# A selective-scan kernel: softplus operations moved by a step, one product with B moved from GpSimd to VectorE, and D times u written by ScalarE instead of TensorE

## The chip, the cores and the metric

The kernel runs on one core of one Trainium2 chip. The metric is the time of one execution on the device in microseconds (us); a kernel's time is the median of its runs. TensorE is the matmul engine, VectorE, ScalarE and GpSimd are the elementwise engines, and SyncE (SP) issues the DMAs. In rows of the profile they are PE (PEld for weight loads), DVE, ACT, POOL and SP.

## The reference, cut to what matters

The input is 4 images of 512 channels of 24 x 24. After a norm over the channels each image becomes a sequence of 2304 steps with 128 channels, one learned token ahead of it, and goes through a Mamba block: 256 inner channels, 16 states each. The second part normalizes again, mixes 8 routed memory blocks into the first 128 tokens and adds.

```python
xz = jnp.einsum('bld,ed->ble', seq, in_proj_w)
u, z = jnp.split(xz, 2, axis=-1)
u = sum((up[:, k:k + L, :] * conv_w[:, k] for k in range(D_CONV))) + conv_b
u = jax.nn.silu(u)
x_dbl = jnp.einsum('bld,ed->ble', u, x_proj_w)
dt, Bm, Cm = jnp.split(x_dbl, [DT_RANK, DT_RANK + D_STATE], axis=-1)
dt = jax.nn.softplus(jnp.einsum('blr,dr->bld', dt, dt_proj_w) + dt_proj_b)
A = -jnp.exp(A_log)

def step(h, inputs):
    dt_t, B_t, C_t, u_t = inputs
    dA = jnp.exp(dt_t[:, :, None] * A)
    h = dA * h + (dt_t * u_t)[:, :, None] * B_t[:, None, :]
    y = jnp.einsum('bdn,bn->bd', h, C_t)
    return (h, y)
...
y = ys.transpose(1, 0, 2) + u * D
y = y * jax.nn.silu(z)
return jnp.einsum('bld,ed->ble', y, out_proj_w)
...
x = x + _L0_conv_ref(_ln_c(x), ...)
t = _to_tokens(x)
t = t + _L0_ffn_ref(_ln_t(t), ...)
```

## The kernel before

**Units and steps.** The work is cut into 24 units: 6 chunks of 4 image rows (384 sequence steps, `T`) times 4 images. The partitions hold 128 channels, and the 256 inner channels lie in two halves, so a tile is 128 x 384 or, for both halves, 128 x 768. Every engine has its own program, written out by hand as 16 steps `s` for each unit `J`, one for each state `n`. In the steps of unit `J` the state work of that unit runs, and beside it the preparation of unit `J + 1` ("front": projections, softplus), the end of unit `J - 1` ("back": output projection, second norm, store) and the first norm of unit `J + 3` ("norm"). Each engine works through its own list in order, and semaphores tie them.

**A state's way through the engines.** ScalarE writes the decay exp(dt A) of each half to `DA` in PSUM (L510) after the scan of that half of the state before it is done, since there is one buffer; states 1 and 2 have theirs written ahead, to `DAS1` and `DAS2` (L518). The drive, dt u times B, is made in one of two ways. For most states TensorE spreads B's row over the partitions into one of two `BB` buffers (L748), one or two steps ahead, and VectorE multiplies (L1057). For `POOL_STATES` = 3, 5, 7, 9 GpSimd does it (L450, in step `n - 2`), from `BS`, which a DMA fills once a unit (`load_b`). VectorE runs the scan of both halves (L1092) in step `n`. In step `n + 1` GpSimd multiplies the states by C (L442), which DMAs bring in groups of four states (`load_c`). In step `n + 3` (`LAG`) TensorE adds the product into `Yp` (L766).

**The turn of the unit.** State 15's product is GpSimd's in step 0 of the next unit and TensorE's in step 2. In step 2 VectorE forms `VV`, `Yp` times silu(z) (L1068), which empties `Yp`; only then may TensorE start the next unit's sum, in step 3. D times u is added to `Yp` by TensorE in step 10, with a diagonal matrix `DD` (L772).

**Softplus.** ScalarE does it in steps 6 to 10 (L589 to L606, absolute value, exp, ln, square, ln) and raises `log_ready`. GpSimd waits for that in step 10 and multiplies `SE` by `SR` (L455); in step 11, after C's product of state 10, it makes dt (L463) and dt times u (L465), and before them XC2 times `RSTD2` (L458), the last product of the second norm. In step 12 it adds the residual (L468), in step 15 it runs the first norm of a later unit (L425).

**The other work of TensorE in the last steps.** In step 12 it projects z (L889), which ScalarE copies from `PP` to `ZB` (L618); the convolution of unit `J + 2` (L907) in steps 13 to 15 uses the same banks and waits for that copy. For the unit before, the output projection (L791, L794) runs in step 3, ScalarE copies it (L546), a mean follows in step 5 (L799), VectorE subtracts it into `XC2` (L1132), ScalarE squares that in step 7 (L621), and TensorE takes the variance in step 8 (L809).

**The last units.** In unit 21 the router's scores are computed (L814, L825, L1102 and others); in units 22 and 23 the routed blocks are mixed by TensorE (L847).

SP issues in every unit: `load_c` for states 4 to 7, the write of the next unit's B and C rows to DRAM, `load_c` for 8 to 11 and 12 to 15, `load_b` and the first `load_c` of the next unit, and the store of the unit before. Each `load_c` waits for the products that free its half of the ring (the one for states 12 to 15 for that of state 7).

Of the kernel before, what the change touches and what calls it, by code (L numbers as in the profile page):

```python
# [11 lines left out]
ACT = mybir.ActivationFunctionType  # L12
ALU = mybir.AluOpType
# [27 lines left out]

FIT_X, FIT_V, FIT_S, FIT_A, FIT_K = 0.50996051, -3.6873482, -0.046276752, 0.88316448, 0.72962086
FIT_BIAS = (1.0, FIT_V, FIT_A, math.log(FIT_K))
POOL_STATES = (3, 5, 7, 9)
NPOOL = len(POOL_STATES)
NDVE = NS - NPOOL
HRING, MRING, CRING = 8, 4, 8
# [20 lines left out]
def build(nc, x, tok, w_in, conv_w, conv_b, xp_w, dt_w, dt_b, a_log, dvec, op_w, mem, router, out):  # L68
    ctx = ExitStack()
    with ctx:  # L70
# [118 lines left out]
        da_ready = sem("da_ready"); das_ready = sem("das_ready"); scan_done = sem("scan_done"); car_saved = sem("car_saved")  # L189
        m_ready = sem("m_ready"); ysum_done = sem("ysum_done")  # L190
        z_ready = sem("z_ready"); z_copied = sem("z_copied")
        gz_ready = sem("gz_ready"); v_ready = sem("v_ready")
        op_ready = sem("op_ready"); x2_ready = sem("x2_ready")
        mean2_ready = sem("mean2_ready"); xc2_ready = sem("xc2_ready"); sq2_ready = sem("sq2_ready")
        var2_ready = sem("var2_ready"); ln2_done = sem("ln2_done"); rstd2_ready = sem("rstd2_ready")
# [82 lines left out]
        def _(sp):  # L278
# [36 lines left out]
            def load_b(unit, p):  # L315

                sp.wait_ge(rows_written, 16 * (unit + 1))
                rows = ROWS_D[p, POOL_STATES[0]:POOL_STATES[-1] + 1:2]
                sp.dma_start(BS[:, :, :], rows.unsqueeze(0).broadcast_to([P, NPOOL, T])).then_inc(bs_loaded, 16)

            def store(c, b, k):
# [68 lines left out]
        @block.gpsimd  # L390
        def _(pool):
            pool.memset(DTNAT, 0.0).then_inc(zeroed, 1)
            pool.memset(MEANW[:, :], 1.0 / DIM).then_inc(const_ready, 1)
            pool.memset(IDENT[:, :], 0.0).then_inc(zeroed, 1)
            pool.memset(EPSC[:, :], EPS_C).then_inc(const_ready, 1)
            pool.memset(EPST[:, :], EPS_T).then_inc(const_ready, 1)
            pool.memset(LOGB[:, 0:1], 2.0 / LOG_C).then_inc(const_ready, 1)
            pool.memset(LOGB[:, 1:2], -LOG_G).then_inc(const_ready, 1)
            for i, v in enumerate(FIT_BIAS):
                pool.memset(FITB[:, i:i + 1], v).then_inc(const_ready, 1)  # L400
            pool.wait_ge(zeroed, 2)
            pool.affine_select(out=IDENT[:, :], in_=IDENT[:, :], compare_op=ALU.not_equal, fill=1.0,
                               base=0, pattern=[[-1, P]], channel_multiplier=1).then_inc(ident_ready, 1)
            pool.memset(XDT0[:, :], 1.0).then_inc(const_ready, 1)
            pool.memset(XDT[:, :], 1.0).then_inc(const_ready, 1)
            pool.memset(ONE4[:, :], 1.0).then_inc(const_ready, 1)
            for b in range(BATCH):
                pool.memset(XN[:, b * SLOT:b * SLOT + HIST - 1], 0.0).then_inc(const_ready, 1)

            pool.memset(SEL[:, :, :], 0.0).then_inc(zeroed, 1)  # L410
            for part in range(PARTS):
                pool.wait_ge(zeroed, 3 + part)
                pool.affine_select(out=SEL[:, :, :], in_=SEL[:, :, :], compare_op=ALU.not_equal, fill=1.0,
                                   base=-part * BC, pattern=[[-1, NS], [0, P]], channel_multiplier=1)\
                    .then_inc(zeroed if part < PARTS - 1 else sel_ready, 1)

            pool.wait_ge(w_loaded, 16 * N_WLOADS)
            for b in range(BATCH):
                pool.tensor_copy(XN[:, b * SLOT + HIST - 1:b * SLOT + HIST], TKC).then_inc(const_ready, 1)

            def normalize(g):

                pool.wait_ge(rstd_ready, g + 1)
                for r1 in range(2):
                    pool.tensor_tensor(seq_rows(unit_seq(g), r1), by_row_parity(XC[:, :, :], r1),  # L425
                                       by_row_parity(over_q(RSTD[:, :]), r1), ALU.mult).then_inc(xn_part, 1)
                pool.wait_ge(xn_part, 2 * (g + 1))
                pool.tensor_copy(XN[:, ds((g + BATCH) * SLOT, HIST)],
                                 XN[:, ds(g * SLOT + T, HIST)]).then_inc(xn_ready, 1)

            def step(J, par, s, main, front, back, prev, conv, norm):
                f, k, g, N = J + 1, J - 1, J + 3, NS * J + s
                fp = kp = 1 - par
                if main and (s > 0 or prev) or (s == 0 and prev):

                    n1 = (s - 1) % NS
                    unit1 = J if s else J - 1
                    g1 = n1 // GRP
                    pool.wait_ge(scan_done, 2 * N)
                    pool.wait_ge(c_loaded[g1 % 2], 16 * (GROUPS // 2 * unit1 + g1 // 2 + 1))  # L440
                    positive(pool, ysum_done, N - MRING)
                    pool.tensor_tensor(M[:, n1 % MRING], HB[:, n1 % HRING],  # L442
                                       over_halves(CS[:, n1 % CRING]), ALU.mult).then_inc(m_ready, 1)
                if main and s + 2 in POOL_STATES:

                    n2 = s + 2
                    pool.wait_ge(bs_loaded, 16 * (J + 1))
                    pool.wait_ge(dtu_ready, J + 1)
                    pool.wait_ge(car_saved, 4 * BATCH + 4 * J + (n2 - HRING) // GRP + 1)
                    pool.tensor_tensor(HB[:, n2 % HRING], DTU[:, par], over_halves(BS[:, pool_index(n2)]),  # L450
                                       ALU.mult).then_inc(dbu_pool, 1)
                if front and s == 10:

                    pool.wait_ge(log_ready, f + 1)
                    pool.tensor_tensor(SE[:, :, :], SE[:, :, :], SR[:, :, :], ALU.mult).then_inc(tail_done, 1)  # L455
                if back and s == 11:
                    pool.wait_ge(rstd2_ready, k + 1)
                    pool.tensor_tensor(XC2[:, :, :], XC2[:, :, :], over_q(RSTD2[:, :]), ALU.mult)\  # L458
                        .then_inc(xh2_done, 1)
                if front and s == 11:  # L460
                    pool.wait_ge(tail_done, f + 1)
                    pool.wait_ge(relu_done, f)
                    pool.tensor_tensor(DT[:, fp], DT[:, fp], SE[:, :, :], ALU.subtract).then_inc(dt_ready, 1)  # L463
                    pool.wait_ge(dt_ready, f + 1)
                    pool.tensor_tensor(DTU[:, fp], DT[:, fp], U[:, fp], ALU.mult).then_inc(dtu_ready, 1)  # L465
                if back and s == 12:
                    pool.wait_ge(xh2_done, k + 1)
                    pool.tensor_tensor(unit_seq(k).rearrange("p (q t) -> p q t", q=Q), XC2[:, :, :], unit_x(k),  # L468
                                       ALU.add).then_inc(out_ready, 1)
                if norm and s == 15:  # L470

                    normalize(g)

            normalize(0)
            normalize(1)
            normalize(2)
            run_units(pool, step)


        @block.scalar  # L480
        def _(act):
# [39 lines left out]
            def step(J, par, s, main, front, back, prev, conv, norm):  # L521
# [17 lines left out]
                if norm and s == 10:  # L539
                    act.wait_ge(xc_ready, g + 1)  # L540
                    positive(act, var_ready, g)
                    act.activation(SQ[:, :, :], XC[:, :, :], ACT.Square).then_inc(sq_ready, 1)
                if back and s == 4:

                    act.wait_ge(op_ready, k + 1)
# [69 lines left out]
                if main and s == z_step(J, norm) + (0 if norm or at(J, ROUTE) else 1):  # L615

                    act.wait_ge(z_ready, J + 1)
                    act.activation(ZB[:, :, :], PPT, ACT.Copy).then_inc(z_copied, 1)  # L618
                if back and s == 7:
                    act.wait_ge(xc2_ready, k + 1)  # L620
                    act.activation(SQ2[:, :, :], XC2[:, :, :], ACT.Square).then_inc(sq2_ready, 1)  # L621
                if back and s == (11 if main and not norm and not front or at(J, COMB - 1) else 9):
                    act.wait_ge(var2_ready, k + 1)
                    act.activation(LNV2[:, :], STAT2, ACT.Ln, bias=EPST[:, 0:1]).then_inc(ln2_done, 1)
# [114 lines left out]
        def _(pe):  # L739
# [4 lines left out]
            def spread_b(unit, par, n):  # L744

                before = NDVE * unit + dve_index(n)
                positive(pe, dbu_dve, before - 1)
                pe.matmul(BB[:, dve_index(n) % 2, 0:T], SEL[:, n], PT[:, par], start=True, stop=True)\  # L748
                    .then_inc(b_ready, 1)

            def step(J, par, s, main, front, back, prev, conv, norm):
# [7 lines left out]
                if main and s >= LAG or prev and s < LAG:  # L759

                    n3 = (s - LAG) % NS
                    pe.wait_ge(m_ready, N - LAG + 1)
                    if s == LAG:
                        positive(pe, v_ready, J)
                    for h in range(HALVES):
                        last = pe.matmul(Yp[:, h, 0:T], IDENT[:, :], M[:, n3 % MRING, h],  # L766
                                         start=n3 == 0, stop=n3 == NS - 1)
                    last.then_inc(ysum_done, 1)
                if main and s == 10:

                    for h in range(HALVES):
                        pe.matmul(Yp[:, h, 0:T], DD[:, h], U[:, par, h], start=False, stop=False)  # L772

                if front and s == 2:

# [255 lines left out]
        def _(dve):  # L1031
# [19 lines left out]
            def drive(unit, par, n, N):  # L1051
# [2 lines left out]
                product = DA[:, :, 0:T] if n in AHEAD else HB[:, n % HRING]  # L1054
                dve.wait_ge(car_saved, 4 * BATCH + 4 * unit + (n - HRING) // GRP + 1)
                dve.wait_ge(b_ready, NDVE * unit + dve_index(n) + 1)
                dve.tensor_tensor(product, DTU[:, par], over_halves(BB[:, dve_index(n) % 2, 0:T]), ALU.mult)\  # L1057
                    .then_inc(dbu_dve, 1)

            def step(J, par, s, main, front, back, prev, conv, norm):  # L1060
# [160 lines left out]
```

## Time and profile before

| | before |
|---|---|
| median of 3 runs | 1181.12 us (1179.61 to 1181.26) |
| the profiled execution's own time | 1184.08 us |
| its span, first to last instruction | 1181.9 us |
| busy: POOL, PE, DVE, ACT | 1062.0, 1043.8, 1024.6, 806.7 us |
| mean granted TensorE clock | 0.971 of full |

Times in rows are us from the span's start unless marked ns. A timeline row gives the start, the duration, the engine, the line, the operation, output and inputs, the count of instructions merged into the row, and in brackets how long the engine was idle before it and what ended that. Elementwise instructions of one engine overlap a little, so that the step from start to start is shorter than a duration.

### The profile page before, as it was taken

How to read it: one execution, taken by the hardware profiler on the slowest of the kernel's cores; microseconds unless marked ns; L12 is line 12 of the kernel's file. 1: busy time of each engine (PE TensorE's matmuls, PEld its weight loads, DVE VectorE, ACT ScalarE, POOL GpSimd, SP SyncE). 2: the span in 40 equal slices, each digit the busy share in tenths (PEclk: the TensorE clock that was granted, in tenths of full speed). 3: DMA queues.
4: the chain of work that ended last, by engine and by line, in shares of the span. 5: the costliest groups of instructions: out<-in, count | busy, mean ns of one | idle time of the engine just before them, and what ended most of it. 6: DMA issues, size and time to landing. Idle time of an engine off the chain costs nothing.

```text
span 1181.9 us, 13090 instructions
## 1 busy us (share of the span) xinstructions
PE 1043.8 (88%) x3786; PEld 616.3 (52%) x3786; DVE 1024.6 (87%) x1173; ACT 806.7 (68%) x1486; POOL 1062.0 (90%) x700
## 2 busy tenths in 40 slices
PE   6889889989998898898899899988988988987987
PEld 4545555555554555555555555555555555544554
DVE  3799898898898898998988988989989889888784
ACT  4677677677676776776766766767767767657653
POOL 3599999999999999999999999999999999978774
PEclk9799999999999999999999999999999999989999
DMA  6223132222322222221322223222322223245441
GB/s 177 93 97 108 63 114 82 89 80 89 115 82 88 95 102 89 88 108 63 114 76 96 82 87 114 82 89 87 109 89 88 105 66 123 87 142 175 154 141 28
DMA packets 64537, 116.78 MB, mean 99 GB/s; under 512 B 34218, under 2 KB 47954, under 8 KB 64466
## 3 DMA queue, kind: packets, MB, share of 16 engines
q1 hardware_dynamic: 64466, 115.96, 29.6%
q8 instruction: 30, 0.49, 0.2%
q14 instruction: 41, 0.34, 0.1%
HBM read 108.47 MB, written 7.47 MB: 98 GB/s over the span
## 4 chain that ended last, share of the span: by engine, by line
POOL 39%; PE 28%; issue 21%; DVE 10%; ACT 1%; POOLq 1%; DMA 0%; DVEq 0%; SPq 0%; ACTq 0%
POOL SCAN L442 28%; PE Yp L766 14%; DVE SCAN L1092 7%; PE PP L907 7%; POOL SCAN L450 6%; POOL UDT L463 3%; PE PP L847 2%; POOL XC L458 2%; DVE SCAN L1057 1%; PE BB L748 1%; PE PP L947 1%; POOLq L255 1%; DVE SCAN L1035 0%; PE PP L809 0%; POOL UDT L465 0%
## 5 line engine op out<-in xcount | busy, mean ns | idle before, releaser
L442 POOL TENSOR_TENSOR SCAN<-SCAN,CS 128x768 f32<-128x768 f32 x384 | 689.3, 1815 | 28.8 <-DVE SCAN L1092 28.0
L1092 DVE TENSOR_TENSOR_SCAN SCAN<-DA,CAR,SCAN 128x384 f32<-128x384 f32 x672 | 639.1, 998 | 3.6 <-POOL SCAN L450 2.0
L766 PE MATMUL Yp<-SCAN,IDENT 128*128 128x384 f32 x1536 | 571.8, 497 | 55.5 <-POOL SCAN L442 54.8
L510 ACT ACTIVATE DA<-UDT,A 128x384 f32<-128x384 f32 x672 | 388.1, 582 | 297.2 <-DVE SCAN L1092 297.2
L766 PEld LDWEIGHTS Yp<-SCAN,IDENT 128*128 128x128 f32 x1536 | 278.4, 191 | 247.8 <-POOL SCAN L442 88.0
L1057 DVE TENSOR_TENSOR SCAN<-UDT,BB 128x768 f32<-128x768 f32 x240 | 222.5, 927 | 10.3 <-PE BB L748 10.2
L450 POOL TENSOR_TENSOR SCAN<-UDT,BS 128x768 f32<-128x768 f32 x96 | 173.9, 1811 | 0.0
L907 PE MATMUL PP<-XN,WT 128*128 128x384 f32 x352 | 137.4, 526 | 2.5 <-ACT ZB L618 1.4
L907 PEld LDWEIGHTS PP<-XN,WT 128*128 128x128 f32 x352 | 71.5, 208 | 64.3 <-issue 29.8
L748 PE MATMUL BB<-PT,SEL 96*128 96x384 bf16 x288 | 94.4, 328 | 1.9 <-DVE DA L1057 1.9
L1068 DVE TENSOR_TENSOR VV<-Yp,GZ 128x768 f32<-128x768 f32 x24 | 23.0, 957 | 69.5 <-PE Yp L766 69.5
L455 POOL TENSOR_TENSOR GATES<-GATES 128x768 f32<-128x768 f32 x23 | 41.7, 1814 | 38.6 <-ACT GATES L606 38.6
L1057 DVE TENSOR_TENSOR DA<-UDT,BB 128x768 f32<-128x768 f32 x48 | 46.2, 962 | 20.8 <-PE BB L748 18.7
L425 POOL TENSOR_TENSOR XN<-XC,RSTD 128x192 f32<-128x192 f32 x48 | 26.8, 581 | 29.1 <-ACT RSTD L670 29.1
L809 PE MATMUL PP<-SQ,MEANW 128*128 128x96 f32 x192 | 26.4, 281 | 28.7 <-ACT SQ L621 28.6
L532 ACT ACTIVATE UDT<-PP,conv_bias 128x384 f32<-128x384 f32 x46 | 26.4, 580 | 35.2 <-PE PP L907 34.9
L1092 DVE TENSOR_TENSOR_SCAN SCAN<-GATES,CAR,DA 128x384 f32<-128x384 f32 x48 | 46.1, 1001 | 0.9
L748 PEld LDWEIGHTS BB<-PT,SEL 96*128 96x128 bf16 x288 | 31.1, 108 | 29.2 <-issue 4.6
L1092 DVE TENSOR_TENSOR_SCAN SCAN<-DAS,CAR,DA 128x384 f32<-128x384 f32 x48 | 45.8, 995 | 0.0
L809 PEld LDWEIGHTS PP<-SQ,MEANW 128*128 128x128 f32 x192 | 23.3, 191 | 42.1 <-issue 39.7
L465 POOL TENSOR_TENSOR UDT<-UDT 128x768 f32<-128x768 f32 x23 | 41.7, 1811 | 1.8
L463 POOL TENSOR_TENSOR UDT<-UDT,GATES 128x768 f32<-128x768 f32 x23 | 41.7, 1812 | 0.0
(203 smaller groups left out, 1134.9 us busy)
## 6 DMA issues: line engine op xcount, KB each, us to landing
CS<-bc_rows SPq DMA_DIRECT2D x96, 768.0 KB, 4.1
BS<-bc_rows SPq DMA_DIRECT2D x24, 768.0 KB, 6.0
out<-XN SPq DMA_DIRECT2D x32, 192.0 KB, 4.2
X<-in_x SPq DMA_DIRECT2D x24, 192.0 KB, 3.5
X<-in_L_ffn_memory_tokens SPq DMA_DIRECT2D x16, 256.0 KB, 3.0
XN<-in_L_ffn_memory_tokens SPq DMA_DIRECT2D x16, 256.0 KB, 3.1
bc_rows<-XDT SPq DMA_DIRECT2D x24, 48.0 KB, 1.5
X<-in_L_ffn_memory_router SPq DMA_DIRECT2D x1, 512.0 KB, 4.4
```

The source lines that it names most:

```text
L442: pool.tensor_tensor(M[:, n1 % MRING], HB[:, n1 % HRING], over_halves(CS[:, n1 % CRING]), ALU.mult).then_inc(m_ready, 1)
L450: pool.tensor_tensor(HB[:, n2 % HRING], DTU[:, par], over_halves(BS[:, pool_index(n2)]), ALU.mult).then_inc(dbu_pool, 1)
L455: pool.tensor_tensor(SE[:, :, :], SE[:, :, :], SR[:, :, :], ALU.mult).then_inc(tail_done, 1)
L463: pool.tensor_tensor(DT[:, fp], DT[:, fp], SE[:, :, :], ALU.subtract).then_inc(dt_ready, 1)
L465: pool.tensor_tensor(DTU[:, fp], DT[:, fp], U[:, fp], ALU.mult).then_inc(dtu_ready, 1)
L510: act.activation(DA[:, h, 0:T], DT[:, par, h], ACT.Exp, scale=A[:, h, n:n + 1])\
L748: pe.matmul(BB[:, dve_index(n) % 2, 0:T], SEL[:, n], PT[:, par], start=True, stop=True)\
L766: last = pe.matmul(Yp[:, h, 0:T], IDENT[:, :], M[:, n3 % MRING, h], start=n3 == 0, stop=n3 == NS - 1)
L809: last = pe.matmul(STAT2, MEANW[:, :], SQ2[:, q], start=q == 0, stop=q == Q - 1)
L907: last = pe.matmul(PP[:, h, 0:T], WT[:, h, tap], XN[:, ds((J + 2) * SLOT + tap, T)], start=tap == 0, stop=tap == TAPS - 1)
L1057: dve.tensor_tensor(product, DTU[:, par], over_halves(BB[:, dve_index(n) % 2, 0:T]), ALU.mult)\
L1092: dve.tensor_tensor_scan(HB[:, s % HRING, h], factor, term, CAR[:, ds(J * NS * HALVES + s * HALVES + h, 1)], ALU.mult, ALU.add).then_inc(s ...
```

## The change

`POOL_STATES` becomes 3, 6, 9: GpSimd has three products with B, and VectorE 13 instead of 12; the `BB` buffers alternate over units. `load_b` gets a wait for the unit's last GpSimd product with B. On GpSimd, SE times SR goes from step 10 to step 11, behind C's product of state 10, and XC2 times `RSTD2` from step 11 to step 12. ScalarE squares XC2 in step 6 instead of step 7. From unit 1 on ScalarE writes D times u to `Yp` in step 2, after VV, ahead of state 3's decays, and TensorE adds all 16 products to it (no `start`); TensorE's `DD` matmuls stay in unit 0 alone, there ahead of the first sum.

```diff
-POOL_STATES = (3, 5, 7, 9)
+POOL_STATES = (3, 6, 9)
...
                 sp.wait_ge(rows_written, 16 * (unit + 1))
-                rows = ROWS_D[p, POOL_STATES[0]:POOL_STATES[-1] + 1:2]
+                positive(sp, dbu_pool, NPOOL * unit)
+                rows = ROWS_D[p, POOL_STATES[0]:POOL_STATES[-1] + 1:POOL_STATES[1] - POOL_STATES[0]]
...
-                if front and s == 10:
+                if front and s == 11:
 
                     pool.wait_ge(log_ready, f + 1)
                     pool.tensor_tensor(SE[:, :, :], SE[:, :, :], SR[:, :, :], ALU.mult).then_inc(tail_done, 1)
-                if back and s == 11:
-                    pool.wait_ge(rstd2_ready, k + 1)
-                    pool.tensor_tensor(XC2[:, :, :], XC2[:, :, :], over_q(RSTD2[:, :]), ALU.mult)\
-                        .then_inc(xh2_done, 1)
-                if front and s == 11:
                     pool.wait_ge(tail_done, f + 1)
...
                 if back and s == 12:
+                    pool.wait_ge(rstd2_ready, k + 1)
...
+                if main and s == LAG - 1 and not at(J, 0):
+
+                    act.wait_ge(v_ready, J)
+                    for h in range(HALVES):
+                        last = act.activation(Yp[:, h, 0:T], U[:, par, h], ACT.Copy, scale=DV[:, h:h + 1])
+                    last.then_inc(du_ready, 1)
+                if back and s == 6:
+                    act.wait_ge(xc2_ready, k + 1)
+                    act.activation(SQ2[:, :, :], XC2[:, :, :], ACT.Square).then_inc(sq2_ready, 1)
...
-                if back and s == 7:
-                    act.wait_ge(xc2_ready, k + 1)
-                    act.activation(SQ2[:, :, :], XC2[:, :, :], ACT.Square).then_inc(sq2_ready, 1)
...
-                pe.matmul(BB[:, dve_index(n) % 2, 0:T], SEL[:, n], PT[:, par], start=True, stop=True)\
+                pe.matmul(BB[:, (NDVE * unit + dve_index(n)) % 2, 0:T], SEL[:, n], PT[:, par], start=True, stop=True)\
...
-                    if s == LAG:
-                        positive(pe, v_ready, J)
+                    if s == LAG and at(J, 0):
+                        for h in range(HALVES):
+                            pe.matmul(Yp[:, h, 0:T], DD[:, h], U[:, par, h], start=True, stop=False,
+                                      skip_group_check=True)
+                    elif s == LAG:
+                        pe.wait_ge(du_ready, J)
                     for h in range(HALVES):
                         last = pe.matmul(Yp[:, h, 0:T], IDENT[:, :], M[:, n3 % MRING, h],
-                                         start=n3 == 0, stop=n3 == NS - 1)
+                                         start=False, stop=n3 == NS - 1,
+                                         skip_group_check=True)
                     last.then_inc(ysum_done, 1)
-                if main and s == 10:
-
-                    for h in range(HALVES):
-                        pe.matmul(Yp[:, h, 0:T], DD[:, h], U[:, par, h], start=False, stop=False)
```

## Rows read from the trace of the kernel before

**Rows 1.** The page: busy time of each engine, and by engine the chain that ended last.

```profile
PE 1043.8 (88%) x3786; PEld 616.3 (52%) x3786; DVE 1024.6 (87%) x1173; ACT 806.7 (68%) x1486; POOL 1062.0 (90%) x700
...
POOL 39%; PE 28%; issue 21%; DVE 10%; ACT 1%; POOLq 1%; DMA 0%; DVEq 0%; SPq 0%; ACTq 0%
```

**Rows 2.** Timeline of VectorE: VV (L1068), scans (L1092), products with B (L1057).

```profile
92.08 0.96 DVE L1068 TENSOR_TENSOR VV<-Yp,GZ 128x768 f32<-128x768 f32 x1 [1.93 <-PE Yp L766]
...
506.71 0.96 DVE L1068 TENSOR_TENSOR VV<-Yp,GZ 128x768 f32<-128x768 f32 x1 [2.78 <-PE Yp L766]
507.59 1.91 DVE L1092 TENSOR_TENSOR_SCAN SCAN<-DAS,CAR,DA 128x384 f32<-128x384 f32 x2
509.41 0.93 DVE L1057 TENSOR_TENSOR SCAN<-UDT,BB 128x768 f32<-128x768 f32 x1
510.26 3.73 DVE L1092 TENSOR_TENSOR_SCAN SCAN<-DA,CAR,SCAN 128x384 f32<-128x384 f32 x4
...
527.60 1.92 DVE L1092 TENSOR_TENSOR_SCAN SCAN<-DA,CAR,SCAN 128x384 f32<-128x384 f32 x2
...
552.05 0.96 DVE L1068 TENSOR_TENSOR VV<-Yp,GZ 128x768 f32<-128x768 f32 x1 [3.26 <-PE Yp L766]
...
1012.27 0.96 DVE L1068 TENSOR_TENSOR VV<-Yp,GZ 128x768 f32<-128x768 f32 x1 [2.77 <-PE Yp L766]
```

**Rows 3.** Timeline of GpSimd around softplus and the turn of the unit.

```profile
502.02 3.58 POOL L442 TENSOR_TENSOR SCAN<-SCAN,CS 128x768 f32<-128x768 f32 x2
505.55 1.81 POOL L450 TENSOR_TENSOR SCAN<-UDT,BS 128x768 f32<-128x768 f32 x1
...
509.57 1.82 POOL L442 TENSOR_TENSOR SCAN<-SCAN,CS 128x768 f32<-128x768 f32 x1 [0.44 <-DVE SCAN L1092]
...
531.07 1.81 POOL L455 TENSOR_TENSOR GATES<-GATES 128x768 f32<-128x768 f32 x1 [1.96 <-ACT GATES L606]
...
539.22 1.81 POOL L442 TENSOR_TENSOR SCAN<-SCAN,CS 128x768 f32<-128x768 f32 x1
...
548.59 3.58 POOL L442 TENSOR_TENSOR SCAN<-SCAN,CS 128x768 f32<-128x768 f32 x2
```

**Rows 4.** Timeline of ScalarE in the same unit.

```profile
512.82 0.49 ACT L546 ACTIVATE X<-PP 128x384 f32<-128x384 f32 x1
...
530.07 0.92 ACT L606 ACTIVATE GATES<-GATES,FITB 128x768 f32<-128x768 f32 x1
...
535.43 0.79 ACT L618 ACTIVATE ZB<-PP 128x768 f32<-128x768 f32 x1
```

**Rows 5.** Timeline of TensorE in that unit and, first row, in the unit before.

```profile
496.45 3.28 PE L907 MATMUL PP<-XN,WT 128*128 128x384 f32 x6
...
541.09 1.56 PE L766 MATMUL Yp<-SCAN,IDENT 128*128 128x384 f32 x4 [2.38 <-POOL SCAN L442]
542.48 2.10 PE L907 MATMUL PP<-XN,WT 128*128 128x384 f32 x6
544.42 0.33 PE L748 MATMUL BB<-PT,SEL 96*128 96x384 bf16 x1
544.58 1.45 PE L766 MATMUL Yp<-SCAN,IDENT 128*128 128x384 f32 x4
545.87 1.46 PE L907 MATMUL PP<-XN,WT 128*128 128x384 f32 x4
```

**Rows 6.** Stretches: us, busy PE, PEld, DVE, ACT, POOL, TensorE clock, DMA, GB/s.

```profile
491.60:495.00 3.40, 1.01 (x5) 0.33 (x3) 3.40 (x5) 2.03 (x6) 3.40 (x3) 1.00 0.00 0
495.00:498.40 3.40, 3.40 (x8) 1.74 (x7) 3.18 (x4) 2.91 (x6) 3.40 (x3) 0.56 0.85 262
```

**Rows 7.** Groups by line: count, busy us, mean ns, idle before and its releaser.

```profile
L510 ACT ACTIVATE DA<-UDT,A 128x384 f32<-128x384 f32 x672 | 388.1, 582 | 297.2 <-DVE SCAN L1092 297.2
...
L809 PE MATMUL PP<-SQ,MEANW 128*128 128x96 f32 x192 | 26.4, 281 | 28.7 <-ACT SQ L621 28.6
```

**Rows 8.** Timeline of VectorE in unit 21, at the router's first step.

```profile
1031.18 0.18 DVE L1102 TENSOR_TENSOR SQ<-X,PP 128x16 f32<-128x16 f32 x1 [2.10 <-PE PP L814]
```

More of the change, by code:

```diff
@@ L191, in build @@
         z_ready = sem("z_ready"); z_copied = sem("z_copied")
-        gz_ready = sem("gz_ready"); v_ready = sem("v_ready")
+        gz_ready = sem("gz_ready"); v_ready = sem("v_ready"); du_ready = sem("du_ready")
         op_ready = sem("op_ready"); x2_ready = sem("x2_ready")
@@ L466, in step @@
                 if back and s == 12:
+                    pool.wait_ge(rstd2_ready, k + 1)
+                    pool.tensor_tensor(XC2[:, :, :], XC2[:, :, :], over_q(RSTD2[:, :]), ALU.mult)\
+                        .then_inc(xh2_done, 1)
+                if back and s == 13:
                     pool.wait_ge(xh2_done, k + 1)
@@ L1056, in drive @@
                 dve.wait_ge(b_ready, NDVE * unit + dve_index(n) + 1)
-                dve.tensor_tensor(product, DTU[:, par], over_halves(BB[:, dve_index(n) % 2, 0:T]), ALU.mult)\
+                dve.tensor_tensor(product, DTU[:, par], over_halves(BB[:, (NDVE * unit + dve_index(n)) % 2, 0:T]), ALU.mult)\
                     .then_inc(dbu_dve, 1)
```

## The prediction

> **What bounds the kernel now.** I read the page's busy shares first: GpSimd is at 90%, TensorE and VectorE just below [rows 1]. The chain that ended last names GpSimd for 39%, but TensorE for 28% too and VectorE for 10%, so no engine bounds alone [rows 1]: there must be a loop that goes through several. One period of it is a unit. The VV products of units 1 and 21 start 920.19 us apart, so 20 units took 46.01 us each [rows 2]. The unit from the VV at 506.71 to that at 552.05 took 45.34 [rows 2], and its neighbours 46.7: two together take 92.0.
>
> The timelines of GpSimd, VectorE and ScalarE side by side give the loop. (a) From VV at 506.71 VectorE hardly waits until state 10's scan ends at 529.52: 22.81 us [rows 2]. (b) ScalarE's last softplus operation, L606, comes behind decay 11, which waits for that scan; it starts at 530.07 and takes 0.92 [rows 4]. GpSimd, idle for 1.96 us then, starts SE times SR at 531.07: 1.55 us after the scan [rows 3]. (c) GpSimd then never waits until C's product of state 15 starts at 548.59: 17.52 us [rows 3]. (d) This product takes 1.8 us and TensorE's sum of it 1.45 us, and VV, for which VectorE has been idle 3.26 us, starts at 552.05: 3.46 us [rows 2, 3, 5]. The sum is 22.81 + 1.55 + 17.52 + 3.46 = 45.34, the whole unit.
>
> In the longer unit (d) is 4.69 instead of 3.46 (502.02 to 506.71), 1.23 more [rows 2, 3]. There six matmuls of L907 take 3.28 us, against 2.10 in the next unit [rows 5]; the granted clock is 0.56 from 495.0 to 498.4, so mostly at 1.2 GHz, right after a stretch in which TensorE was busy for 1.01 of 3.4 us, waiting for GpSimd [rows 6]. TensorE is then behind when state 15 comes.
>
> **The change, part by part, on this loop.**
>
> *Three products with B instead of four.* GpSimd loses one operation of 1.81 us, a step of 1.77 from start to start (two of the like take 3.53 from 502.02 to 505.55) [rows 3]. All its products with B lie early in the unit, in (a), where the loop runs on VectorE. So this removal by itself gives the loop nothing; it makes GpSimd reach state 10 sooner and wait there. VectorE gains one product: states 4, 5, 7, 8, 10, 11 instead of 4, 6, 8, 10, 11 between VV and the scan of 10. One is 0.93 us, 0.85 from start to start [rows 2]. (a) becomes 23.66. TensorE spreads one B more, a 0.33 us matmul that moves its successor by 0.16 (544.42 to 544.58) [rows 5]. Its parity over units only keeps the two BB buffers alternating now that 13 is odd. B's load shrinks by a quarter, and it has half a unit to land.
>
> *The load's new wait.* On SP it is behind the third load of C, which waits for C's product of state 7; GpSimd issues that behind its last product with B, so the new wait is always already met. Behind it in SP's queue are the next unit's first C load and the store; neither moves for it.
>
> *Softplus in step 11.* Now C's product of state 10 comes first and starts 0.07 us after the scan (like the product that waited at 509.57 for a scan ending at 509.50) [rows 2, 3]. It covers 1.77 us, and L606 is ready after 1.55, so SE times SR finds it there, with 0.2 to spare. The operations from there to state 15's product are those of (c) in another order (XC2 times RSTD2 too is still among them): 17.52 stays. So (b) goes from 1.55 to 0.07. If that cover is gone (ScalarE later by over 0.2 us) the excess comes back.
>
> *Square of XC2 in step 6.* It leaves the packed ScalarE steps between softplus operations; XC2 is written before state 6's scan, so no decay waits for it longer. TensorE's wait for it, 28.6 us over 22 units or 1.3 each [rows 7], goes. Outside the last units it is off the loop.
>
> *D times u by ScalarE.* Two scaled copies SBUF to PSUM, 128x384. The trace has no such one; the nearest are the decays, same route and size, 0.58 us each, and below them L546 with 0.49, PSUM to SBUF [rows 4, 7]. I take the decay's, so 1.2 us for both (1.0 by the other). They start when VV ends, at +1.0 from its start, and end at +2.2. Queued behind them is state 3's decay, which already had to wait for the first half of a scan, until 508.6 or +1.9 [rows 2]: it slips some 0.3 us, and VectorE needs it only at +3.55 (510.26) [rows 2], so nothing. TensorE's first sum of the unit waits too: it goes from just over +1.0 to +2.2. Behind it are the output projection, the sums of states 1 and 2, and the mean that XC2 on VectorE needs. ScalarE reads the projection (L546) at 512.82, +6.1, without idle time ahead of it [rows 4], so the projection lay there; how long, the row doesn't say. The bounds for XC2's delay are 0 and the whole 1.2; I take 0, since ScalarE comes to L546 by its own order, behind decays. TensorE loses the 4 DD matmuls, as large as the 4 of a sum, 1.45 us [rows 5], off the loop in full units.
>
> The new unit: 23.66 + 0.07 + 17.52 + 3.46 = 44.71 us at full clock. The other limits are below: GpSimd's own steps 42.2 (estimates from one unit's starts: 22 of 1.77, two of 0.96, 1.3 for the norm); VectorE, 45.34 less its 3.26 wait plus 0.85 = 42.9.
>
> *Where the stall goes, and the clock.* TensorE is late next. It sums state 10 until about 3.3 us after the scan; the convolution behind waits for ScalarE's copy of z, which ends 6.7 us after the scan as before (535.43 + 0.79 less 529.52) [rows 4]. The old idle of 2.38 us [rows 5] becomes about 3.4. So low clock will come at least as often, perhaps in 6 units of 10. From 9.0 us after the scan TensorE has four sums of 1.29 (544.58 to 545.87), 3.2 us of convolution (1.94, from 542.48 to 544.42, and 1.3) and 0.5 of B's [rows 5]: it would be done at 17.9, and state 15's product ends at 0.07 + 17.52 + 1.77 = 19.4. Before, its products of 11 and 15 started 9.4 us apart (539.22, 548.59); with XC2's product of 1.0 moved in between it is 10.3 [rows 3]. A low stretch costs up to 1.7 us of work (3.28 less 2.10 in L907, the rest in the sum ahead [rows 5]), so TensorE is at 19.6 or somewhat over: 0.3 to 0.6 late per low stretch, none when it misses. Mean over units: between 0 and 0.6, I take 0.3. The unit is 45.0 us, 1.0 less than 46.01.
>
> The Trainium skill ("TensorE: Matmul & The Clock Gate", Part 1) says that the default state is throttled and activity releases the throttle. By that rule idle time that grows speaks against this change; the trace agrees in that the low stretch stands right behind the idle one [rows 6], and with 1.23 in every unit the sum would be the first rival below.
>
> *Ends.* Unit 0 gains (b) less 0.85, 0.6 us. In unit 21 VectorE waits 2.10 us for L814 [rows 8], which stands behind L809 and its 1.3 us wait for the square; with that gone, and 0.85 of the 2.10 taken by the product added, some 1.2 comes back. Units 22 and 23 run on TensorE with the routed mixing: the DD matmuls, 1.3 us a unit, go, VectorE gets 0.85; between +1.7 and -2.6 together, I take -0.1.
>
> Sum: 20 x 1.0 + 0.6 + 1.2 + 0.1 = 22 us. The profiled execution took 1184.08 us for a span of 1181.9 (the table), 3.0 over the median of the runs; I take the difference off the median, 1181.12 - 22 = 1159.
>
> **Rivals.**
> 1. Low clock at the full old price in every unit: 44.71 + 1.23 = 45.94. Gain 20 x 0.07 + 2 = 3.4, 1178 us. For it: the longer idle. Against: the extra time between states 11 and 15. Chance 0.10.
> 2. Slower: the longer idle brings low clock in two stretches of every unit, with TensorE behind by 2 x 1.23: 47.2 us, plus 24 less 2, 1203 us. It decides from 1.4 us per unit (46.01 + 0.1 - 44.71). Against: the idle is one gap, and before there was never more than one such stretch in a unit. Chance 0.08.
> 3. D times u is on the path: sum, projection and XC2 slip by the full 1.2 us, and scan 10 with them: 44.7 to 45.0 becomes 45.9 to 46.2, between 4 of gain and 2 of loss, 1179 us. Against: the slack shown. Chance 0.07.
> 4. The softplus wait stays in part, since ScalarE is late by 1 us: 45.7 to 46.0 us, some 1175 us. The change would not do what it says. Chance 0.07.
> 5. GpSimd alone was the bound, by its 90%: each unit gives 1.77, so 35 + 2, 1144 us. Against: its idle 1.96 us [rows 3], and (a). Chance 0.08.
> 6. The forecast: 0.60, its own range 1153 (no low stretch costs anything) to 1165 (0.6 each).
>
> The range must leave out no more than 2 in 10. Below 1149 is most of rival 5; above 1178 is rival 2 and part of 1 and 3. So 1149 to 1178. About 0.2% (2.4 us) is what a measurement can tell from no change. Slower: rival 2 and little else, 0.09. Within 0.2%: halves of 1 and 3, 0.08. Faster: 0.83.
>
> **What the new profile would show.** VV to VV near 44.7 to 45.3 us. GpSimd waits some 1.6 us before C's product of state 10 for VectorE's scan, and none before SE times SR. VectorE's wait for VV falls from about 3 to about 2 us. TensorE idles some 3.4 us before the convolution, for ScalarE's copy; L907 behind it is slow in about half of the units. State 3's decay starts at about +2.1 from VV. It would be wrong if VV stood over 3.5 us behind the start of state 15's product in most units, if SE times SR still waited, or if VectorE waited for the mean ahead of XC2.

## The result and the profile after

The changed kernel takes 1154.86 us (median of 4 runs, 1153.59 to 1155.36), against 1181.19 before; the ratio is 0.977, with a 95% interval of 0.975 to 0.979. That is 26.3 us less, where 22 were forecast (1159). The span of the profiled execution is 1151.8 us.

The page, busy time and chain, to be read beside [rows 1]:

```profile
PE 1006.2 (87%) x3718; PEld 588.6 (51%) x3718; DVE 1044.1 (91%) x1197; ACT 831.5 (72%) x1532; POOL 1023.6 (89%) x676
...
PE 34%; POOL 28%; DVE 21%; issue 13%; ACT 3%; POOLq 0%; DMA 0%; DVEq 0%; SPq 0%; ACTq 0%
```

GpSimd lost 38 us of work, and the kernel 26; VectorE gained 20 us of work and is now the busiest. VectorE's part of the last chain has doubled. The timelines of one unit show the loop. VectorE, as in [rows 2]:

```profile
88.24 0.96 DVE L1075 TENSOR_TENSOR VV<-Yp,GZ 128x768 f32<-128x768 f32 x1 [0.57 <-PE Yp L776]
...
490.53 0.96 DVE L1075 TENSOR_TENSOR VV<-Yp,GZ 128x768 f32<-128x768 f32 x1 [1.99 <-PE Yp L776]
...
500.41 0.54 DVE L1139 TENSOR_TENSOR XC<-X,PP 128x384 f32<-128x384 f32 x1
...
512.12 1.92 DVE L1099 TENSOR_TENSOR_SCAN SCAN<-DA,CAR,SCAN 128x384 f32<-128x384 f32 x2
...
535.24 0.96 DVE L1075 TENSOR_TENSOR VV<-Yp,GZ 128x768 f32<-128x768 f32 x1 [2.02 <-PE Yp L776]
...
982.19 0.96 DVE L1075 TENSOR_TENSOR VV<-Yp,GZ 128x768 f32<-128x768 f32 x1 [2.00 <-PE Yp L776]
```

GpSimd, as in [rows 3]:

```profile
514.13 1.82 POOL L443 TENSOR_TENSOR SCAN<-SCAN,CS 128x768 f32<-128x768 f32 x1 [1.32 <-DVE SCAN L1099]
515.90 1.82 POOL L456 TENSOR_TENSOR GATES<-GATES 128x768 f32<-128x768 f32 x1
517.80 1.81 POOL L459 TENSOR_TENSOR UDT<-UDT,GATES 128x768 f32<-128x768 f32 x1
...
525.94 1.02 POOL L468 TENSOR_TENSOR XN<-XC,X 128x384 f32<-128x384 f32 x1
...
531.79 3.57 POOL L443 TENSOR_TENSOR SCAN<-SCAN,CS 128x768 f32<-128x768 f32 x2
```

ScalarE, as in [rows 4], at the turn of the unit and at the copy of z:

```profile
491.53 1.09 ACT L547 ACTIVATE Yp<-UDT,DV 128x384 f32<-128x384 f32 x2 [2.47 <-DVE VV L1075]
492.55 0.56 ACT L510 ACTIVATE DA<-UDT,A 128x384 f32<-128x384 f32 x1
...
517.28 0.32 ACT L620 ACTIVATE LNV<-PP,EPSC 128x96 f32<-128x96 f32 x1
...
519.97 0.79 ACT L627 ACTIVATE ZB<-PP 128x768 f32<-128x768 f32 x1
```

TensorE, as in [rows 5], at the turn and from z's projection to the sum of state 11:

```profile
492.76 1.53 PE L776 MATMUL Yp<-SCAN,IDENT 128*128 128x384 f32 x4 [0.81 <-ACT Yp L547]
...
517.75 1.53 PE L896 MATMUL PP<-XN,WZT 128*128 128x384 f32 x4 [1.17 <-ACT LNV L620]
519.12 0.33 PE L754 MATMUL BB<-PT,SEL 96*128 96x384 bf16 x1
519.28 1.45 PE L776 MATMUL Yp<-SCAN,IDENT 128*128 128x384 f32 x4
520.90 2.17 PE L914 MATMUL PP<-XN,WT 128*128 128x384 f32 x6 [0.17 <-ACT ZB L627]
522.91 0.33 PE L754 MATMUL BB<-PT,SEL 96*128 96x384 bf16 x1
523.32 1.56 PE L776 MATMUL Yp<-SCAN,IDENT 128*128 128x384 f32 x4
524.71 2.10 PE L914 MATMUL PP<-XN,WT 128*128 128x384 f32 x6
```

The unit from 490.53 to 535.24 is 23.51 us to the end of state 10's scan (514.04), 0.09 to GpSimd's product of it, 17.66 to the product of state 15 and 3.45 to VV: 44.71. From the VV of unit 1 to that of unit 21 it is 893.95 us, 44.70 per unit, and the units no longer alternate: the six matmuls of L907 (now L914), 3.28 in every second unit before [rows 5], take 2.10.

The spans of the two profiled executions differ by 30.1 us. The 20 units give 26.2 of them, unit 0 gives 0.5, and 3.4 lie ahead of state 0's first scan (it starts at 40.4, against 43.8). In that start TensorE's granted clock was low from about 27 to 41 us before, and not after: eight matmuls of L947 (now L954) take 5.49 us before and 2.85 after. Of the experiments below, e1, e2, e7 and e8 have 7 to 14 us of low clock there, and the others have none. Each kernel has one traced execution, so it is not shown that the change has to do with it. The medians differ by 26.3 us only, since the profiled execution was 2.9 us over the median before and 1.3 us under it after. How these 26.3 divide is therefore known only roughly.

The change also moves the residual add (L468) from step 12 to step 13, which the description ahead left out: in the rows it stands behind the product of state 12. It stays between the products of states 10 and 15, so the sum is the same.

### The profile page after: what moved, and what is told of

Its sections match the earlier page's. It is cut to its first block, busy times and chain, and to the rows that moved or that the text cites. A ratio compares the mean times of both kernels' runs of the same rounds, so it can differ in the third digit from the quotient of the medians.

```text
span 1151.8 us, 13023 instructions
## 1 busy us (share of the span) xinstructions
PE 1006.2 (87%) x3718; PEld 588.6 (51%) x3718; DVE 1044.1 (91%) x1197; ACT 831.5 (72%) x1532; POOL 1023.6 (89%) x676
## 4 chain that ended last, share of the span: by engine, by line
PE 34%; POOL 28%; DVE 21%; issue 13%; ACT 3%; POOLq 0%; DMA 0%; DVEq 0%; SPq 0%; ACTq 0%
PE Yp L776 18%; POOL SCAN L443 15%; DVE SCAN L1099 13%; DVE SCAN L1064 4%; POOL GATES L456 3%; POOL UDT L459 3%; PE PP L798 3%; PE PP L854 2%; ACT Yp L547 2%; DVE VV L1075 2%; POOL XN L426 2%; PE PP L806 2%; POOL XC L464 2%; POOL XN L468 2%; PE PP L936 2%
## 5 line engine op out<-in xcount | busy, mean ns | idle before, releaser
L776 PE MATMUL Yp<-SCAN,IDENT 128*128 128x384 f32 x1536 | 564.5, 492 | 43.6 <-POOL SCAN L443 23.3
L1064 DVE TENSOR_TENSOR SCAN<-UDT,BB 128x768 f32<-128x768 f32 x264 | 247.5, 937 | 6.8 <-PE BB L754 6.7
L754 PE MATMUL BB<-PT,SEL 96*128 96x384 bf16 x312 | 103.2, 331 | 34.8 <-DVE SCAN L1064 31.2
L451 POOL TENSOR_TENSOR SCAN<-UDT,BS 128x768 f32<-128x768 f32 x72 | 130.5, 1813 | 0.0
L914 PE MATMUL PP<-XN,WT 128*128 128x384 f32 x352 | 126.0, 490 | 4.8 <-ACT ZB L627 4.8
L914 PEld LDWEIGHTS PP<-XN,WT 128*128 128x128 f32 x352 | 64.8, 189 | 58.8 <-issue 17.7
L547 ACT ACTIVATE Yp<-UDT,DV 128x384 f32<-128x384 f32 x46 | 25.0, 576 | 55.5 <-DVE VV L1075 55.5
L896 PE MATMUL PP<-XN,WZT 128*128 128x384 f32 x96 | 36.5, 503 | 26.7 <-ACT LNV L620 24.6
L1064 DVE TENSOR_TENSOR DA<-UDT,BB 128x768 f32<-128x768 f32 x48 | 46.2, 962 | 1.6
L798 PE MATMUL PP<-VV,OPT 128*128 128x192 f32 x192 | 38.3, 342 | 3.6 <-DVE XN L1055 2.5
```

What stands on the lines that cost most here:

```text
L754: pe.matmul(BB[:, (NDVE * unit + dve_index(n)) % 2, 0:T], SEL[:, n], PT[:, par], start=True, stop=True)\
L798: pe.matmul(PP[:, 0, r1 * 2 * TOK:(r1 + 1) * 2 * TOK], OPT[:, h], VV[:, h].rearrange("p (h r w s) -> p r s h w", h=ROWS, r=2, w=WW)[:, r1] ...
L914: last = pe.matmul(PP[:, h, 0:T], WT[:, h, tap], XN[:, ds((J + 2) * SLOT + tap, T)], start=tap == 0, stop=tap == TAPS - 1)
L1064: dve.tensor_tensor(product, DTU[:, par], over_halves(BB[:, (NDVE * unit + dve_index(n)) % 2, 0:T]), ALU.mult)\
```

## The experiments

The unit of each kernel is the distance between VV products in the steady stretch; before it was 46.01 on average. A low stretch is one in which TensorE's granted clock is at 1.2 GHz; those between units 1 and 21 last 3.4 us each in every trace. Times "by the ratios" compare two kernels through their ratios to the kernel before, of which each batch of runs has its own.

**e1: the GpSimd order alone.** Four products with B, no D times u on ScalarE, the square in step 7.

```diff
-                if front and s == 10:
+                if front and s == 11:
                     pool.wait_ge(log_ready, f + 1)
                     pool.tensor_tensor(SE[:, :, :], SE[:, :, :], SR[:, :, :], ALU.mult).then_inc(tail_done, 1)
...
-                if back and s == 11:
-                    pool.wait_ge(rstd2_ready, k + 1)
-                    pool.tensor_tensor(XC2[:, :, :], XC2[:, :, :], over_q(RSTD2[:, :]), ALU.mult)\
-                        .then_inc(xh2_done, 1)
-                if front and s == 11:
...
                 if back and s == 12:
+                    pool.wait_ge(rstd2_ready, k + 1)
+                    pool.tensor_tensor(XC2[:, :, :], XC2[:, :, :], over_q(RSTD2[:, :]), ALU.mult)\
+                        .then_inc(xh2_done, 1)
+                if back and s == 13:
                     pool.wait_ge(xh2_done, k + 1)
```

> Only the GpSimd order of the change is made (softplus operations in step 11 behind the product of state 10, second norm's product in step 12, residual add in step 13); GpSimd keeps four products with B. Theory of the loop: the 1.55 us between state 10's scan and SE times SR become 0.07, while VectorE has no product more, so the loop is 22.8 + 0.1 + 17.6 + 3.5 = 44.0 us and GpSimd's own steps are 44.0 too: about 44.1 us per unit, 1140 to 1146 us in all, faster than the whole change. Rival (GpSimd's load is what bounds, and the product taken from it is the gain): at least half of the 26 us is missing, 1165 us or more.

Measured: 1147.6 us, ratio 0.970 (0.966 to 0.974); the unit is 44.25, where 44.1 was expected, and the time lies 1.6 us over the expected range. This one part gives more than the whole change. Its GpSimd timeline around state 10 and the next turn:

```profile
506.45 7.15 POOL L442 TENSOR_TENSOR SCAN<-SCAN,CS 128x768 f32<-128x768 f32 x4
513.57 1.81 POOL L455 TENSOR_TENSOR GATES<-GATES 128x768 f32<-128x768 f32 x1
...
529.45 3.57 POOL L442 TENSOR_TENSOR SCAN<-SCAN,CS 128x768 f32<-128x768 f32 x2
```

No row of that unit has idle time: here, and only from here on, GpSimd's load is the bound. The rival (the product taken away is the gain) falls.

**e2: the B part alone**, with `load_b`'s rows and wait as in the change.

```diff
-POOL_STATES = (3, 5, 7, 9)
+POOL_STATES = (3, 6, 9)
...
-                pe.matmul(BB[:, dve_index(n) % 2, 0:T], SEL[:, n], PT[:, par], start=True, stop=True)\
+                pe.matmul(BB[:, (NDVE * unit + dve_index(n)) % 2, 0:T], SEL[:, n], PT[:, par], start=True, stop=True)\
```

> Only the B part of the change is made (states 3, 6, 9 on GpSimd, buffers alternating over units). Theory of the loop: VectorE's extra 0.85 us lies on it and GpSimd's operation does not, so the unit is 46.2 us at full clock and up to 47 with low stretches: same or slower, 1181 to 1195 us. Rival (GpSimd's load bounds): 1.77 us less in every unit, 1140 to 1150 us.

Measured: 1224.66 us, ratio 1.036 (1.032 to 1.039). Taking an operation of 1.8 us per unit from the busiest engine made the kernel 43 us slower, 30 us over the expected range. Three of the 20 units take 46.22, as the sum said (46.19), but 14 take 47.88, with one low stretch each, and three 49.1, with two. In a unit of 49.1, its rows, VectorE, then TensorE, then two stretches with the granted clock:

```profile
545.67 0.56 DVE L1079 TENSOR_TENSOR XC<-X,PP 128x384 f32<-128x384 f32 x1 [1.71 <-PE PP L868]
```

```profile
540.56 2.00 PE L810 MATMUL PP<-SQ,MEANW 128*128 128x96 f32 x8 [2.23 <-ACT SQ L622]
542.34 0.53 PE L749 MATMUL BB<-PT,SEL 96*128 96x384 bf16 x1
542.66 2.11 PE L767 MATMUL Yp<-SCAN,IDENT 128*128 128x384 f32 x4
544.61 1.03 PE L868 MATMUL PP<-X,MEANW 128*128 128x96 f32 x8
```

```profile
537.50:540.50 3.00, 0.82 (x3) 0.19 (x1) 3.00 (x5) 2.81 (x6) 3.00 (x3) 1.00 0.00 0
540.50:543.90 3.40, 3.34 (x11) 2.81 (x12) 3.40 (x4) 3.08 (x7) 3.27 (x3) 0.51 0.48 184
```

The new drive of state 7 makes ScalarE, which goes scan by scan, reach the square of XC2 later. TensorE idles 2.23 us for it and works at 1.2 GHz behind that; the mean L868 is late, and VectorE waits 1.71 us for it just ahead of state 10's scan, in (a), where nothing hides it.

**e3: the changed kernel with four products on GpSimd.** Only `POOL_STATES` is edited; it is (3, 5, 7, 9) again.

> The changed kernel with four products with B on GpSimd again (states 3, 5, 7, 9), 12 on VectorE. Theory of the loop: 0.65 us less per unit than the changed kernel, from 44.7 to 44.0 or 44.1, so 1140 to 1143 us. Rival (GpSimd's load bounds): up to 1.8 us per unit more than the changed kernel, up to 1190 us.

Measured: 1145.25 us, ratio 0.970 (0.966 to 0.973), 9.6 us below the changed kernel (9 by the ratios) and 2 us over the expected range; the unit is 44.22, and GpSimd has no idle time in it, as in e1. So of the change as it stands the B part is a loss of 0.48 us per unit: less than the 0.85 of the drive, because with four products GpSimd bounds at 44.2.

**e4: the changed kernel without D times u on ScalarE.** The ScalarE write goes, the DD matmuls stand in step 10 again.

```diff
-                if main and s == LAG - 1 and not at(J, 0):
-
-                    act.wait_ge(v_ready, J)
-                    for h in range(HALVES):
-                        last = act.activation(Yp[:, h, 0:T], U[:, par, h], ACT.Copy, scale=DV[:, h:h + 1])
-                    last.then_inc(du_ready, 1)
...
+                if main and s == 10:
+
+                    for h in range(HALVES):
+                        pe.matmul(Yp[:, h, 0:T], DD[:, h], U[:, par, h], start=False, stop=False)
```

> The changed kernel with D times u by TensorE's DD matmuls in step 10 again, and no ScalarE write. Theory: ScalarE's write costs nothing in the full units and the DD matmuls gain nothing there; the last two units lose up to 2.6 us: 1155 to 1158 us, 44.7 us per unit. Rival A (the write delays VectorE through the projection and the mean): 1 us less per unit, 1135 us. Rival B (four fewer matmuls are what keeps TensorE from falling behind): low clock or late sums come back and the unit is 45.3 us or more, 1167 us or more.

Measured: 1157.17 us, ratio 0.980 (0.977 to 0.983), 2.3 us over the changed kernel (3 by the ratios, whose intervals overlap, so this size is uncertain). The unit is 44.70, the same; in units 21 to 23 the distances are 52.6, 56.7 and 50.5, against 51.4, 56.1 and 49.1. Both rivals fall.

**e5: the changed kernel with the square in step 7.** Only ScalarE's square of XC2 goes back to its old place in the list, behind the copy of z.

```diff
-                if back and s == 6:
-                    act.wait_ge(xc2_ready, k + 1)
-                    act.activation(SQ2[:, :, :], XC2[:, :, :], ACT.Square).then_inc(sq2_ready, 1)
...
+                if back and s == 7:
+                    act.wait_ge(xc2_ready, k + 1)
+                    act.activation(SQ2[:, :, :], XC2[:, :, :], ACT.Square).then_inc(sq2_ready, 1)
```

> The changed kernel with the square of XC2 in step 7 as before. Theory of the prediction (the square is off the loop in full units): 44.7 us per unit, only unit 21 loses up to 1.2 us, so 1155 to 1157 us. Theory after the run with the B part alone (with the extra drives the square comes 2.2 us after TensorE is ready for it, the low clock follows and the mean for XC is late by 1.7 us in front of state 10's scan): the unit is up to 46.4 us, 1175 to 1190 us.

Measured: 1168.11 us, ratio 0.991 (0.987 to 0.994), 13 us over the changed kernel (16 by the ratios): half of the gain is gone. TensorE waits 48.0 us in 22 units for the square, as in e2. Most units take 44.86 and every third or fourth 46.5; in one of these, TensorE, then VectorE:

```profile
240.53 1.10 PE L816 MATMUL PP<-SQ,MEANW 128*128 128x96 f32 x8 [2.23 <-ACT SQ L627]
...
245.66 0.56 DVE L1085 TENSOR_TENSOR XC<-X,PP 128x384 f32<-128x384 f32 x1 [1.74 <-PE PP L874]
```

There are five such units and, between units 1 and 21, five low stretches in the record of the granted clock, each right behind a wait of 2.23 us for the square. The first theory, that of the prediction, falls: the square is on the loop once the B part is in. The second is right in kind and too high in size (1175 us was its least), since the low stretch comes in one unit of four only.

**e6: the B part and the square in step 6.**

> The kernel before with the B part and the square of XC2 in step 6, softplus and D times u as before. If the late square is what made the B part alone cost 43 us, and not the drive itself: the unit is the predicted 46.2 us at full clock, up to 46.8 with the old low stretches at the turn of the unit, 1183 to 1196 us. Rival (the drive, or the buffers' new parity, costs it): 47.9 us per unit, 1218 us or more.

Measured: 1201.21 us, ratio 1.019 (1.016 to 1.022), 23 us less than e2 (20 by the ratios) for the place of one operation. The units are 46.04 and 47.25, three of four the longer; that is the predicted 46.2, and 1.2 more where the low stretch at the turn of the unit comes, which it does more often than before. It missed its range, 1183 to 1196, by 5 us for that reason.

**e8: the idle time ahead of the sum of state 11 filled.** The kernel before with fillers on TensorE. They write to Yp's bank while the sum runs there, and the kernel's output is wrong, so it stands for its time alone.

```diff
+                if main and norm and s == 14:
+                    for i in range(12):
+                        pe.matmul(Yp[:, 0, 384:512], IDENT[:, :], MEANW[:, :], start=True, stop=True, skip_group_check=True)
```

> The kernel before with 12 idle matmuls of 128 columns (their results lie in unused columns of Yp's bank and are never read) in step 14 of units 0 to 20, ahead of TensorE's wait for the product of state 11, where it idles 2.4 us. If that idle time is what the low clock stands behind, and the low clock the 1.23 us of every second unit: all units 45.3 us, no low stretch at the turn, 1166 to 1171 us. Rival (the low clock has another cause, or the longer units do): 1180 us or more, units still alternating.

Measured: 1175.01 us, ratio 0.994 (0.991 to 0.996). Every unit takes 45.35 to 45.50 us; the alternation is gone, and from unit 1 to 21 the record of the granted clock has no low stretch. TensorE at the place where it was idle for 2.4 us, first the fillers, then the sum of state 11:

```profile
534.62 2.84 PE L761 MATMUL Yp<-MEANW,IDENT 128*128 128x128 f32 x24
537.30 1.46 PE L769 MATMUL Yp<-SCAN,IDENT 128*128 128x384 f32 x4
```

Units at the low price, 46.7, have become units of 45.5: that is 0.53 per unit on average, 10.7 us over 20. The spans show 9.1 of them (1181.9 and 1172.8), the medians 5.6, and 1175 us lies over the expected range. The kernel before was traced in an execution 3.4 us over the median of its runs here, so with more low clock than most (0.971 granted, against up to 0.978); the full 10.7 us hold for that execution.

**e7: the logarithm ahead of the decays.** What e1 and e3 point to: GpSimd's 1.32 us wait for scan 10 in the changed kernel can be filled if the logarithm does not itself wait for that scan.

```diff
+                if front and s == 9:
+
+                    act.wait_ge(sp_chain, 4 * f + 3)
+                    act.activation(SR[:, :, :], SR[:, :, :], ACT.Square, bias=FITB[:, 1:2]).then_inc(sp_chain, 1)
+                if front and s == 10:
+
+                    act.wait_ge(sp_chain, 4 * f + 4)
+                    act.activation(SR[:, :, :], SR[:, :, :], ACT.Ln, bias=FITB[:, 2:3], scale=FIT_S)\
+                        .then_inc(log_ready, 1)
                 if norm and s == 10:
                     act.wait_ge(xc_ready, g + 1)
...
-                if front and s == 11:
+                if front and s == 10:
 
                     pool.wait_ge(log_ready, f + 1)
                     pool.tensor_tensor(SE[:, :, :], SE[:, :, :], SR[:, :, :], ALU.mult).then_inc(tail_done, 1)
+                if front and s == 11:
```

(The two operations leave their old places behind the decays.)

> The changed kernel with ScalarE's last two softplus operations put ahead of the decays of steps 9 and 10, and GpSimd's SE times SR back in step 10, ahead of the product of state 10. Theory of the loop: the logarithm is ready at about the end of GpSimd's product of state 9, so GpSimd's 1.3 us wait for state 10's scan is filled with SE times SR and the loop through scan 10 falls below VectorE's own work: 42.9 to 43.4 us per unit, 1120 to 1130 us. Rival A (the decays moved back delay scans 10 and 11): up to 1 us per unit lost, 1155 to 1175 us. Rival B (GpSimd's wait only moves to the product of state 11 or later): 44.7 us, 1155 us.

Measured: 1133.98 us, ratio 0.961 (0.958 to 0.964), the fastest of all; the unit is 43.68, somewhat over the expected 42.9 to 43.4, and the time is 4 us over the expected range. GpSimd around state 10, and VV:

```profile
503.88 1.81 POOL L456 TENSOR_TENSOR GATES<-GATES 128x768 f32<-128x768 f32 x1 [0.43 <-ACT GATES L547]
505.65 1.81 POOL L443 TENSOR_TENSOR SCAN<-SCAN,CS 128x768 f32<-128x768 f32 x1
```

```profile
524.85 0.96 DVE L1076 TENSOR_TENSOR VV<-Yp,GZ 128x768 f32<-128x768 f32 x1 [0.98 <-PE Yp L777]
```

SE times SR still waits 0.43 us for the logarithm, now the term of the loop in the place of scan 10: VV at 481.19, 22.69 to SE times SR, 17.51 to state 15's product (521.39), 3.46 to VV (524.85).

**e9: e7 with four products on GpSimd.**

> The kernel with the logarithm ahead of the decays, with four products with B on GpSimd (states 3, 5, 7, 9) instead of three. Theory: with the loop through scan 10 out of the way GpSimd's own work bounds again, the same 44.2 us per unit as with four products and the order of the change, 1143 to 1147 us; so the product taken from GpSimd pays 0.5 us per unit here, while with the order of the change it cost 0.5. Rival (the loop still runs through state 10's scan, where one drive fewer is 0.85 us less): 42.9 us per unit, 1120 us or less.

Measured: 1139.91 us, ratio 0.966 (0.962 to 0.969), 5.9 us over e7 and 3 us under the expected range; the unit is 44.11. GpSimd bounds again, without idle time in the unit, at nearly the 44.2 of e3 and e1, and the rival falls. So the product moved to VectorE costs 0.48 us per unit in the changed kernel and gives 0.43 in e7.

## Why the prediction was right, and where it was not

The mechanism was right, and so was its size in full units: 44.71 at full clock worked out, 44.70 measured. To agree within 0.01 is partly luck, since (a) came out 0.15 shorter and (c) 0.14 longer.

(a) VV to the end of scan 10: 23.66 said, 23.51 measured. That the extra drive counts here and GpSimd's product for nothing is shown by the undisturbed units of e2, 46.22 against 45.34. GpSimd waits 1.32 us ahead of state 10's product (1.6 said), and 0.52 ahead of state 6's, which was not said.

(b) 0.07 said, 0.09 measured. SE times SR starts right behind the product, without a wait. e1 shows this part alone.

(c), (d) 17.52 and 3.46 said, 17.66 and 3.45 measured.

D times u: two writes of together 1.09 us, state 3's decay at +2.02, TensorE's first sum at +2.23, and XC2 at +9.88 (500.41), exactly where it was (516.59 less 506.71). The value 0 for XC2's delay was right; e4 shows the same unit without the write. What it gives is 2.3 us by the medians, outside the full units. That these lie in the last units is read from one execution each.

**The step that failed: "The old idle of 2.38 us becomes about 3.4. So low clock will come at least as often", and with it the 0.3 us per unit, 6 us too much in the sum.** No low stretch came between units 1 and 21. I had TensorE sum state 10 at once and then wait for ScalarE's copy of z. In its order z's projection stands ahead of that sum, and it waits for ScalarE's L620, which comes behind decay 12 and so behind scan 11: the projection starts 3.7 us after scan 10, the sum at 5.2 (worked out as ending at 3.3), the convolution at 6.9, the next sum at 9.3. So the time in which TensorE waits is cut into pieces of 1.17, 0.17 and 0.08 us with matmuls between. That TensorE's idle time of 2.4 us is what the low clock stood behind is shown by e8, where filling it took every low stretch and the 46.7 us units away; and e5, which puts a wait of 2.2 us in one piece into the changed kernel, has low stretches again. The Trainium skill ("TensorE: Matmul & The Clock Gate", Part 1) says that activity releases the throttle, and e8 agrees; it was my account of where the idle time goes that was wrong. Rivals 1 and 2 hung on it.

The forecast was 4.3 us too high and not 6 for reasons that were not foreseen. In the profiled pair unit 21 gave 1.3 us more than said and the start 3.4 that no term had, the last two units lost 2.5, and the pair stands 4.2 us further apart than the medians. That these nearly cancel is chance.

**A second step that failed: "Outside the last units it is off the loop", of the square in step 6.** e5 shows 13 us for it. In its trace 8.2 us are the low stretches of five units (46.5 against 44.86), 3.2 us are 0.16 in each of the 20 units, which was not followed up, and 1.2 us are in unit 21 (52.6 against 51.4), the one place where the prediction had put it, at this size. e2 against e6 shows 23. The forecast came out right since the change has the square in step 6. My account took TensorE's 1.3 us wait as hidden, which it was; I did not follow what the B part does to it: with a drive more ahead of it the wait becomes 2.2 us, low clock follows, and a mean behind it on TensorE is late for VectorE. Rows of before could have shown the length of that queue: square, variance, B, sum, mean, XC, scan 10.

The ends: 0.6 said for unit 0 and 0.5 measured (from state 0's scan to the first VV 48.3 and 47.8); unit 21 is 2.5 us shorter (53.8 to 51.4; 1.2 said, which e5 finds for the square, and e4 finds as much for D times u), unit 22 the same and unit 23 2.5 longer (46.7 to 49.1; 0.1 less was said for the two together). There TensorE ran the output projection at low clock (2.90 us) and VectorE waited 4.0 us for the mean behind it. What brought that low stretch about was not tried apart.

Rival 5 (GpSimd alone bounds, 1144) is refuted by e2 and e3. Rivals 3 and 4 are refuted by the rows.

## What to carry to other kernels

Before taking work from the busiest engine, write down the loop that one period runs through, engine by engine, and see whether the operation lies on it: here the same product cost 43 us alone (some 20 of them through the late square), cost 10 us in the finished change, and gave 6 once its loop was out of the way. A wait that another wait starts (ScalarE's logarithm behind a decay behind a scan) is worth more than an operation: putting an operation that is ready anyway in front of it cost nothing and gave 34 us alone. When an edit delays an engine that works in lockstep, follow every other operation in its list too, and whoever stands behind the ones that wait.

## What the runs showed of the hardware

The granted clock fell behind waits of TensorE that were shorter than the low stretch that followed: 2.4 us ahead of the sum of state 11 in the kernel before and in e6, 2.23 us at the square in e2 and e5, with 3.4 us at 1.2 GHz behind each. Not every such wait was followed by one. The waits stand in each of the 20 units, and the low stretch came in 10 before, in 15 in e6, in 17 at the square in e2 and in 5 in e5. So such a wait is a cost with a frequency. The kernels differ in their period, but no run changed the period alone, so what sets the frequency is open. No low stretch stood behind the waits of 1.0 to 1.5 us for the square in the full units before and in e1 and e8, nor behind those of up to 1.2 us in the changed kernel.
